# A rebuilt softmax stage with unread matmuls on TensorE, and a linear-attention stage written out without a loop

## The reference, cut to what matters

```python
x = x + _L0_attn_a_ref(_layernorm(x), ..., Wqkv, Wproj, bproj)   # x: (4, 512, 256) f32
x = x + _L0_ffn_ref(_layernorm(x), w1, w3, w2, wr)
x = x + _L0_attn_b_ref(_layernorm(x), Wq, Wk, Wv, Wb, bb, Wg, Wo, ...)
x = x + _L0_ffn_ref(_layernorm(x), w1, w3, w2, wr)

# _L0_attn_a_ref: plain softmax attention, 16 heads of width 16, per batch of 512 tokens
attn = softmax(einsum('gqd,gkd->gqk', q, k) * norm); ctx = einsum('gqk,gkd->gqd', attn, v)
out = ctx @ Wproj.T + bproj
# _L0_attn_b_ref: 16 heads of width 128, a scan over the 512 tokens of each batch
q = layernorm(silu(causal_dwconv(hidden @ Wq, 4 taps)));  k likewise;  v = hidden @ Wv
S = (1 - b) * S + b * (v_t[..., :, None] * k_t[..., None, :]);  o_t = einsum('bhvk,bhk->bhv', S, q_t)
o = o * silu(hidden @ Wg);  return o @ Wo
# _L0_ffn_ref: top-2 of 8 routes, rows added by the route's index; silu(silu(x w1) w3) w2
```

## Time and profile before

| what | value |
|---|---|
| median of 3 runs | 1244.14 us (1239.82 to 1247.75) |
| the profiled execution's own time | 1245.81 us |
| its span, first to last instruction | 1244.0 us |
| mean granted TensorE clock | 0.963 |
| busy: PE, DVE, ACT, POOL | 92%, 74%, 61%, 50% |

### The profile page before, as it was taken

The page is one execution under the profiler, slowest core; times in us unless marked ns, Lnnn a source line. Parts: engine busy times, 40 slices in busy tenths (PEclk is TensorE's granted clock), DMA queues, the critical chain, the costliest instruction groups (busy, mean ns, idle before and its releaser), DMA issues. The chain is left out here.

```text
span 1244.0 us, 22999 instructions
## 1 busy us (share of the span) xinstructions
PE 1146.6 (92%) x7450; PEld 909.6 (73%) x7450; DVE 925.3 (74%) x2112; ACT 760.2 (61%) x1400; POOL 622.1 (50%) x1066
## 2 busy tenths in 40 slices
PE   4799999998687899999999999999999999999768
PEld 3344444434565789998999998999998899999646
DVE  6857777783725688888888887888888788888452
ACT  3146565666243777777677676777677677767423
POOL 5100000000431687787776776687777678676520
PEclk9679999999798999999999999999999999999889
DMA  4312222210302001201211211201211211101020
GB/s 149 72 32 52 53 53 53 52 28 1 118 1 71 30 31 46 79 32 45 65 46 39 71 46 33 78 32 46 65 46 45 65 38 39 46 31 46 16 68 1
DMA packets 26677, 60.90 MB, mean 49 GB/s; under 512 B 5367, under 2 KB 10359, under 8 KB 25399
## 3 DMA queue, kind: packets, MB, share of 16 engines
q1 hardware_dynamic: 26551, 59.34, 15.7%
HBM read 44.15 MB, written 2.33 MB: 37 GB/s over the span
## 5 line engine op out<-in xcount | busy, mean ns | idle before, releaser
L1514 DVE SCALAR_TENSOR_TENSOR l_conv<-l_proj_q,par,l_conv 128x511 f32<-128x511 f32 (+2 forms) x192 | 142.4, 742 | 115.7 <-ACT l_conv L1430 112.4
L556 DVE TENSOR_REDUCE a_neg_max<-a_scores 128x1 f32<-128x512 f32 x236 | 154.9, 685 | 66.6 <-PE a_scores L360 66.4
L498 ACT ACTIVATE a_probs<-a_scores_t 128x1024 f32<-128x1024 f32 x128 | 124.3, 1022 | 58.5 <-PE a_scores_t L375 57.7
L1514 DVE SCALAR_TENSOR_TENSOR l_conv<-l_proj_k,par,l_conv 128x511 f32<-128x511 f32 (+2 forms) x192 | 142.8, 744 | 6.4 <-DVE l_conv L1514 0.6
L1256 POOL TENSOR_TENSOR l_k_tok<-l_normed,k_norm 128x384 f32<-128x384 f32 x64 | 65.1, 1016 | 158.4 <-ACT l_normed L1447 158.4
L1436 ACT ACTIVATE l_conv<-l_conv,par 128x512 f32<-128x512 f32 x128 | 92.5, 723 | 84.5 <-DVE l_conv L1514 82.8
L87 POOL MEMSET ln_minus_half_b<- 128x4 f32 x1 | 0.1, 102 | 282.5 <-POOLq L612 282.5
L360 PE MATMUL a_scores<-a_k_stack,a_q_stack 48*128 48x512 f32 x236 | 109.2, 506 | 14.3 <-DVE a_neg_max L556 12.1
L360 PEld LDWEIGHTS a_scores<-a_k_stack,a_q_stack 48*128 48x128 f32 x236 | 42.8, 193 | 105.9 <-DVE a_neg_max L556 88.4
L1447 ACT ACTIVATE l_normed<-l_turn_q,l_shift,l_scale 128x128 f32<-128x128 f32 x256 | 96.5, 458 | 23.1 <-POOL l_shift L1248 23.0
L1246 POOL TENSOR_TENSOR l_scale<-l_small,l_minus_half 128x8 f32<-128x8 f32 x64 | 105.2, 1644 | 5.0
(11 more groups left out here) (292 smaller groups left out, 3515.3 us busy)
## 6 DMA issues: line engine op xcount, KB each, us to landing
l_keep<-keep_rows SPq DMA_DIRECT2D x64, 448.0 KB, 3.5
head_raw<-w_heads SPq DMA_DIRECT2D x8, 1024.0 KB, 6.8
a_q_stack<-a_dense_hi SPq DMA_DIRECT2D x64, 64.0 KB, 2.2
a_k_stack<-a_dense_hi SPq DMA_DIRECT2D x64, 64.0 KB, 2.2
x_tok<-x SPq DMA_DIRECT2D x4, 512.0 KB, 7.0
a_q_stack<-a_dense_lo SPq DMA_DIRECT2D x32, 64.0 KB, 2.2
a_k_stack<-a_dense_lo SPq DMA_DIRECT2D x32, 64.0 KB, 2.2
wo_raw<-w_o SPq DMA_DIRECT2D x1, 2048.0 KB, 11.8
```

The costliest lines, as they stand in the source:

```text
L498: act.activation(probs[:, n % 2, 2 * half:2 * half + 2, :], scores_t[half][:], ACT.Exp, scale=SOFT_SCALE).then_inc(probs_done, 1)
L556: dve.tensor_reduce(neg_max[:, g % 2, at:at + 1], max_bank(g, j), AX.X, ALU.max, negate=True).then_inc(max_done, 1)
L1514: ins = dve.scalar_tensor_tensor(conv[:, w, m, s:], proj[w][:, 0:SEQ - s], par[:, h, tap:tap + 1], conv[:, w, m, s:], ALU.mult, ALU.add)
```

## The change

Softmax attention, in `softmax_attention` and `layer_norm`:

- Chunk n of the probabilities now follows the maxima by `lag = 6` slots, not by 8. There are 70 slots, not 72: 6 with maxima alone, 58 with both, 6 with probabilities alone. A maximum row is now read two slots after its transposition. The 6 banks in turn serve the first 24 tiles (`wide_tiles`), not 32.
- q and k lie in one tensor (`dense`, `stack`), so one DMA carries a part of q and a part of k: 6 DMAs of 128 KB for a quad (`restack`) in place of 12 of 64 KB. The first two wait for the high halves alone.
- SP's order becomes `rows(s-1, 1)`, `rows(s, 0)`, `restack(s+1, 0)`, `restack(s+1, 1)`; the wait for the weights' loads moves from the front of the queue to its end.
- The maxima are split before their transposition, by two small DVE operations on 128 partitions; one transposition and one ACT copy then move both halves, and the 4 row DMAs each carry a high and a low row of one pair.
- Batch 0 alone is normalised and transposed ahead (batch 1 normalised too). Batches 1 to 3 are transposed in slots 6 and 7 of rounds 0, 2 and 4 (`turned_in`), with their high and low halves; the statistics of batches 2 and 3 stand in slot 6 of rounds 1 and 3, their normalising in slot 1 of rounds 2 and 4. `normalise` of batch 0 stands ahead of the low half of the weights.
- In `layer_norm` ACT's high half waits for its own four transpositions, not for all eight. This holds for every stage.
- Unread matmuls: `keep_busy(20)` before the first transposition, `keep_busy(8)` behind it, `keep_busy(10)` before slot 0, and four of 512 columns (`keep_busy_beside`) in each of the slots 0 to 5. They write `ctx_acc`, which the first context call overwrites.

Linear attention: `steps` writes all 8 pairs out, on every engine; no loop is left.

```diff
     def normalise(dve, g):
         dve.wait_ge(rstd_ready, g + 1)
-        if g >= 2:
-            dve.wait_ge(transposed, g - 1)
+        if g >= depth:
+            dve.wait_ge(transposed, KD * (g - depth + 1))
...
+    def high(act, g, k, bank):
+        act.wait_ge(transposed, KD * g + k + 1)
+        act.activation(xn_hi[:, k, g * cols:(g + 1) * cols], bank, ACT.Copy).then_inc(hi_done, 1)
...
+    lag = 6
+    wide_tiles = lag * max_per_chunk
...
-        dense_hi = sb("a_dense_hi", [P, 2, 2, SEQ], F32R)
-        dense_lo = sb("a_dense_lo", [P, 2, 2, SEQ], F32R)
...
+        dense = sb("a_dense", [P, 2, 4, SEQ], F32R)
+        stack = [sb(f"a_stack{i}", [P, HPG // 2, 2, SEQ], F32R) for i in range(2)]
...
+            def restack(g, quad):
...
+                for r, (k_part, q_part) in enumerate(((K_HI, Q_HI), (K_LO, Q_HI), (K_HI, Q_LO))):
+                    sp.wait_ge(dense_lo_done if r else dense_hi_done, 2 * g + 2)
+                    for e in range(2):
+                        at, of = e * HALF_ROWS + r * HN, quad * 4 * HN + e * 2 * HN
+                        sp.dma_start(f32(stack[i][at:at + HN, hs, :, :]),
+                                     f32(dense[of:of + 2 * HN, i, k_part:q_part + 1:q_part - k_part, :])).then_inc(
+                            stacked[i][quad], 16)
...
             for s in range(groups + 1):
                 if s >= 1:
                     rows(s - 1, 1)
-                if s + 1 < groups:
-                    stack(s + 1, 0)
                 if s < groups:
                     rows(s, 0)
                 if s + 1 < groups:
-                    stack(s + 1, 1)
+                    restack(s + 1, 0)
+                    restack(s + 1, 1)
+            sp.wait_ge(w_loaded, 16 * len(loads))
...
+            def keep_busy(count):
+
+                for _ in range(count):
+                    pe.matmul(ctx_acc[:, 0:P], ident[:], ident[:], start=True, stop=True)
+
+            def keep_busy_beside(tiles):
+
+                for _ in range(tiles):
+                    pe.matmul(ctx_acc[:], w_hi[:, 0, 0:P], xn_hi[:, 0, 0:SEQ], start=True, stop=True)
...
+                elif c == 6 and turned_in(s):
...
+                    pe.wait_ge(ln.normed, (turned_in(s) + 1) * TPB)
+                    ln.turn(pe, turned_in(s), 0, misc)
+                elif c == 7 and turned_in(s):
+                    pe.wait_ge(ln.lo_done, KD * turned_in(s) + 1)
+                    ln.turn(pe, turned_in(s), 1, misc)
...
-            pe.wait_ge(ln.lo_done, KD * NB)
-            for s in range(groups + 1):
-                for c in range(chunks):
-                    n = (s - 1) * chunks + c
-                    j = c * max_per_chunk
-                    for half in range(2):
-                        if s >= 1:
-                            probs_chunk(s - 1, c, half)
...
+            keep_busy(10)
+            for slot in range(groups * chunks + lag):
+                s, c, n = slot // chunks, slot % chunks, slot - lag
+                j = c * max_per_chunk
+                for half in range(2):
+                    if n >= 0:
+                        probs_chunk(n // chunks, n % chunks, half)
                     if s < groups:
-                        max_scores(s, j + 2)
...
+                        max_scores(s, j + half)
+                    if n < 0:
+                        keep_busy_beside(1)
+                if n >= 1:
+                    context(n - 1)
...
             def split_max(g, quad):
...
+                dve.tensor_copy(max_parts[:, i, quad, :, 0, :], whole).then_inc(max_hi_done, 1)
                 dve.wait_ge(max_hi_done, quads * g + quad + 1)
...
             dve.wait_ge(x_loaded[0], 16)
             ln.statistics(dve, 0)
+            ln.normalise(dve, 0)
             dve.wait_ge(w_hi_ready, 1)
             dve.tensor_tensor(w_lo[:], w_raw, f32(w_hi[:]), ALU.subtract).then_inc(w_lo_ready, 1)
-            ln.normalise(dve, 0)
+            ln.low_parts(dve, 0)
...
-        def steps(eng, step, lags, last_apart=False):
-
-            for pair in range(2):
+        def steps(step, lags):
+
+            for pair in range(PAIRS):
                 for k in range(BODY):
-                    step(pair, k, pair * BODY + k, pair)
-            with eng.Fori(1, PAIRS // 2 - 1 if last_apart else PAIRS // 2) as couple:
...
+                    step(pair, k, pair * BODY + k, pair % 2)
             for k in range(lags):
                 step(PAIRS, k, UNITS + k, 0)
```

More of the change, by code:

```diff
@@ L99, in normalise, with turn, low @@
         dve.wait_ge(rstd_ready, g + 1)
-        if g >= 2:
-            dve.wait_ge(transposed, g - 1)
+        if g >= depth:
+            dve.wait_ge(transposed, KD * (g - depth + 1))
         for t in range(group):
             n = g * group + t
-            dve.tensor_scalar(xn[:, g % 2, t, :], x_tok[:, n, :], mean_var[:, n, 0:1], rstd[:, n:n + 1],
+            dve.tensor_scalar(xn[:, g % depth, t, :], x_tok[:, n, :], mean_var[:, n, 0:1], rstd[:, n:n + 1],
                               ALU.subtract, ALU.mult).then_inc(normed, 1)
+    def turn(pe, g, k, bank):
+        for t in range(group):
+            last = pe.transpose(bank[:, t * P:(t + 1) * P], xn[:, g % depth, t, k * P:(k + 1) * P], ident[:])
+        last.then_inc(transposed, 1)
+    def high(act, g, k, bank):
+        act.wait_ge(transposed, KD * g + k + 1)
+        act.activation(xn_hi[:, k, g * cols:(g + 1) * cols], bank, ACT.Copy).then_inc(hi_done, 1)
+    def low(dve, g, k, bank):
+        c = slice(g * cols, (g + 1) * cols)
+        dve.wait_ge(hi_done, KD * g + k + 1)
+        dve.tensor_tensor(xn_lo[:, k, c], bank, f32(xn_hi[:, k, c]), ALU.subtract).then_inc(lo_done, 1)
     def transpose(pe, g):
@@ L111, in transpose @@
         for k in range(KD):
[L112 to L115, removed]
+            turn(pe, g, k, xt[g % turns][k])
     def high_parts(act, g):
-        act.wait_ge(transposed, g + 1)
         for k in range(KD):
-            act.activation(xn_hi[:, k, g * cols:(g + 1) * cols], xt[g % turns][k][:], ACT.Copy).then_inc(hi_done, 1)
+            high(act, g, k, xt[g % turns][k][:])
     def low_parts(dve, g):
         for k in range(KD):
[L124 to L127, removed]
+            low(dve, g, k, xt[g % turns][k][:])
     steps = Steps()
     steps.statistics, steps.normalise, steps.low_parts, steps.lo_done = statistics, normalise, low_parts, lo_done
-    steps.normed = normed
+    steps.normed, steps.turn, steps.high, steps.low = normed, turn, high, low
     steps.constants, steps.deviations, steps.transpose, steps.high_parts = constants, deviations, transpose, high_parts
@@ L190, in max_bank, with last_use @@
         def max_bank(g, j):
-            return first_scores[j % len(first_scores)] if g == 0 else scores[j % 2][:]
+            n = g * tiles_per_group + j
+            return first_scores[n % len(first_scores)] if n < wide_tiles else scores[n % 2][:]
+        def last_use(n):
+            turns = len(first_scores)
+            if n < wide_tiles:
+                return n - turns
+            return n - 2 if n >= wide_tiles + 2 else max(i for i in range(wide_tiles) if i % turns == n % 2)
         def half_rows(stack, e, count):
@@ new lines, in rows @@
+            def rows(g, quad):
+                i = g % 2
+                sp.wait_ge(max_copied, quads * g + quad + 1)
+                for e in range(2):
+                    for pair in range(2):
+                        at, of = e * HALF_ROWS + STACK, (2 * e + pair) * 2 * TPB
+                        sp.dma_start(f32(stack[i][at:at + 2, 2 * quad + pair, 1, :]),
+                                     f32(max_rows_t[of:of + 2 * TPB, quad, :])).then_inc(max_rows[quad], 16)
+            restack(0, 0)
@@ L279, in _ @@
+            restack(0, 1)
             for s in range(groups + 1):
@@ L505, in copy_context, with copy_max @@
                 act.activation(ctx_t[:], ctx_acc[:], ACT.Copy).then_inc(ctx_copied, 1)
[L507 removed]
+            def copy_max(g, quad):
                 act.wait_ge(max_t_done, quads * g + quad + 1)
```

221 lines of the change are left out of this document (99 added, 122 removed).

## The result

The changed kernel takes 1256.78 us (median of 11 runs, 1246.74 to 1272.54), the kernel before beside it 1242.23: a ratio of 1.0102, 95% interval 1.0077 to 1.0128, which leaves out the slow run of 1272.54, at a granted clock of 0.942. It is slower by 1%; the forecast was 1226, a gain of 18 us. The profiled execution took 1251.61 us with a span of 1249.8, 5.8 over the span before. The two halves of the change went opposite ways: between the two profiled executions the linear stage won 11.2 us and the softmax stage lost 17.8.

A forecast was written before the change was run, and what follows sets the result against it. PE was taken to bound the softmax rounds, DMA waits and a partly low clock the start. Softmax -6.6 and linear attention -11.1 gave -17.7 against the median 1244.1: 1226 us, range 1214 to 1233 (chance 0.62).

The forecast's parts named there:

- Linear attention: Linear stage: written out, 61 periods of 11.89 us without the loop's stalls, -11.1 us.
- rival (c): Linear stage: straight code stalls as the loop did, 0 in place of -11.1, 1237 us; chance 0.07.
- The ramp, -7.7: First scores to first probabilities: 16.8 us in place of 24.5, with unread products lying beside DVE's work.
- Rival (a): Softmax start: clock stays low up to round 1's end, +19.4 us, about 1245; chance 0.12.
- Round 1 at the high level: -6.5: Softmax round 1: slow for the clock alone, so the high level wins 6.5 us.
- the two extra slots: Softmax: two more slots hold both maxima and probabilities, with four transpositions in each, +7.4 us.
- Up to the first scores: Softmax start: earlier projections, 6 issues instead of 12, 128 KB landing as fast as 64 KB; 21.8 us, -9.7.
- Rounds 2 to 7: Softmax: +12 us in all, from 2.0 for transpositions, 3 for DVE's pieces and 7 for row waits.
- The 7 us of row waits: Softmax slots 2 and 6 of each round: PE waits for a maximum row's DMA, +7 us (bounds 0 and 10).
- The 3 us for DVE's pieces: Softmax rounds: statistics, normalising and low halves moved into them, longer than one slot's room, +3 us (0 to 10).
- The row wait at the end: End of softmax: one wait for a row where slots are only 2.2 us long, +2.3 us.
- Rival (d): SP's queue: larger four-dimensional DMAs issue slower, at 1.57 us each +54 us, about 1280; chance 0.05.

The follow-up runs named there:

- e10: The changed kernel with the linear stage's loops put back (softmax half only); 1261.5 us, ratio 1.0163 to the kernel before.
- e6: e1 with the unread products put between the matmuls of its round 0, four for each chunk; 1254.3 us, ratio 1.0097 to the kernel before.
- e9: The changed kernel with the unread products of slots 0 to 5 on 48 rows, like the scores, instead of 128; 1244.4 us, ratio 1.0015 to the kernel before.
- e2: The changed kernel without the unread products beside the scores in slots 0 to 5; 1237.9 us, ratio 0.9982 to the kernel before.
- e7: e2 with POOL's deviations of batches 0 and 1 ahead of its fills of v_tok; 1237.1 us, ratio 0.9975 to the kernel before.
- e3: The changed kernel with no unread products at all; 1241.8 us, ratio 0.9996 to the kernel before.
- e5: e2 with twelve restack DMAs of 64 KB for a quad in place of six of 128 KB; 1277.5 us, ratio 1.0337 to the kernel before.
- e8: e2 with the layer norm of all four batches ahead of slot 0; 1241.8 us, ratio 1.0004 to the kernel before.
- e4: The changed kernel with 25 unread products ahead of slot 0 in place of 10; 1251.3 us, ratio 1.01 to the kernel before.
- e1: The kernel before with only the linear stage written out; 1230.2 us, ratio 0.9927 to the kernel before.
- e11: e1 again, in five rounds beside the kernel before; 1233.1 us, ratio 0.9947 to the kernel before.

## Why the prediction failed

**Linear attention** was right by its step: straight code with no stall, 61 periods of at most 11.90 (rival (c) fell). The size, -11.1 forecast and -11.2 measured, holds for the profiled execution before, from which it was read. It took in a fall of the clock behind the loop's turns that is not always there: on e10's loop the gain is 6.9, and by the medians 7.4 and 9.6. The forecast was also counted from a median of 1244.1, of 3 runs; 11 gave 1242.2.

**The ramp, -7.7, is where the sign turned.** The step was "The 24 unread products lie beside DVE: a slot holds 8 matmuls of 0.23, 1.85 us, beside DVE's 2.4." The 0.23 is from matmuls of one shape in a run. In alternation with scores of 48 rows each takes 0.43 at the high level, 3.4 us a slot, and 0.72 at the low one, 5.8 (e6). The loads are exposed, and the scores can no longer start in twos (e9). PE, not DVE, set the pace. The level fell as well, and the two multiply. With the high level throughout, 24 pairs of 0.85 and the 12 matmuls of two projections at 0.23 would be 23.2 us (an estimate): 6.4 over the forecast's 16.8 for the interval, and the other 7.9 up to 31.05 for the level. Rival (a) was the right mechanism for the clock, but it priced a slot at the low level at 3.7 us, where it takes 5.8; it gave 1245, and a chance of 0.12.

**"Round 1 at the high level: -6.5"** rested on the clock staying up through round 0. Measured: -1.1. In e2's profiled execution the level was back by 55 us and round 1 took 33.65; in e7's it stayed at 0.50 until some 77 us and round 1 took 40.6. So the 6.5 is there to be had, but not each time. In the changed kernel the two extra slots, 58.82 to 72.89, fell into the second low stretch, 60 to 86 us: 11.35 in place of 7.4.

**Up to the first scores,** 6.0 us less was won than forecast: 3.0 by SP's queue starting at 19.21 in place of 16.2 and 2.9 by the landing. Of the first, DVE's normalising took 1.3 longer (e7), and `keep_busy(8)`, merged to 3.24 us from 12.45 on, held the first projection until 15.45, when the low halves were there at 14.0. Part of this is the execution: in e10, with the same instructions, the eight took 1.95 us, the clock was 1.00 in that stretch for 0.68, and the queue started at 17.39. The forecast had priced the 20 products ahead of the transpositions and none of the eight behind them. That the projections might start low, as it allowed, is seen in full only in e3, which has none of these products; in e5 the first two ran low. The landing was taken "as fast as 64 KB"; it is 5.1 against 2.2 us (e5).

**Rounds 2 to 7** grew by 6.8, not by 12. The 7 us of row waits did not come: a row transposed at 94.05 in slot 4 of round 1 is read at 98.38 after 0.2 us of waiting. The 3 us for DVE's pieces and 2 for the transpositions are together 5.0 in e8's difference. The row wait at the end, where slots are short, is there: 1.85 us at 304.42, for 2.3 forecast.

**Rival (d)** did not come in this kernel: 12 issues took 7.77 us, 0.65 each. e5 shows that its mechanism is real.

What stays open: why the granted clock falls within a few us of the first scores (at 29 in the changed kernel, at 32 in e4 with PE busy throughout, at 27 in e2 without products beside the scores), and why it comes back for good at 55 us in e2 and between 69 and 101 in the other profiles. e3 and e4 show only that neither more nor less filling ahead of the scores keeps it up. The products don't start the fall, but with them the first low stretch is longer: 17 us in the changed kernel, 20 in e4 and 47 in e9, for 7 in e2, 10 in e3 and 14 in e1. In the changed kernel, e2, e3, e4, e9 and e10 the level first came back during the six matmuls of a projection or within 1 us of their end; other projections in the same stretches (e4's of 41.33) did not bring it back. And e2 is still some 6 us slower than e1 and e11 (0.9982 against 0.9937); from round 2 to the end of the stage it takes 207.6 us, they take 201.5. With the norm back ahead of slot 0 (e8) it is 201.2, so these 6 us are the moved layer norm, while e2's earlier start seems to gain nothing in the median run. The last is read from medians and not from a profile of a median run of e2. So even without the products the rebuilt softmax stage loses these 6 us to the one before.

## What to carry to other kernels

Price an unread matmul by the interval it will have between its new neighbours, not by the one it has in a run of its own kind; where the number of rows changed at every matmul, the load of the weights was added in full here (0.29 us at the low level), and matmuls that had run side by side no longer did. A fill costs nothing only if it fits beside the other engine's work at the low clock level too. And when two stages are changed at once, run each alone: here one half was worth 0.6% and hid behind a half that lost 1.6%. The same holds for a size read from a single profile: look at the granted clock at that place, and take a second profile of the same code.

## What the runs showed that I had not expected

- Alternating 48 and 128 rows: 0.43 us a matmul at the high level and 0.72 at the low one, against 0.23 and 0.43 for equal rows; two matmuls on rows 0 to 47 and 64 to 111 start together (33.73 in e2).
- The clock level falls with PE busy 5.00 of 5.00 us (e4), so a full PE was not enough to hold it.
- A stand of PE of 2.1 to 2.5 us at the loop's first turning back was followed by a lower clock in one execution (0.66 in the next 5 us, before) and not in another (1.00, e10); the loop cost 4.3 us more in the first.
- A DMA of 128 KB from SBUF to SBUF lands after 5.1 us, one of 64 KB after 2.2; the DMA engines' share is 1.08 at 130 GB/s with the first and 0.45 at 105 GB/s with the second.
- DVE's normalising of a batch takes 2.71 to 3.09 us beside POOL's fills and 1.38 without them (e7).
